# VectorE's 32x32 turns write adjacent elements with the channel outermost; TensorE reads runs and writes PSUM at a step

## What is computed

```python
def spectral_conv(x, w1, w2):
    x_ft = jnp.fft.rfft2(x)
    out_ft = jnp.zeros((b, w1.shape[1], h, w // 2 + 1), dtype=x_ft.dtype)
    out_ft = out_ft.at[:, :, :M1, :M2].set(jnp.einsum('bixy,ioxy->boxy', x_ft[:, :, :M1, :M2], w1))
    out_ft = out_ft.at[:, :, -M1:, :M2].set(jnp.einsum('bixy,ioxy->boxy', x_ft[:, :, -M1:, :M2], w2))
    return jnp.fft.irfft2(out_ft, s=(h, w))
h = layer_norm(x @ fc0_w + fc0_b, ln0_g, ln0_b)            # the stem
for i in range(LAYERS):                                     # 4 layers, M1 = M2 = 12
    x1 = spectral_conv(h, w1, w2)
    x2 = jnp.einsum('bchw,oc->bohw', h, conv_w[i]) + conv_b[i][None, :, None, None]
    h = layer_norm(x1 + x2, ln_g[i], ln_b[i])               # then gelu, but for the last layer
h = gelu(h @ fc1_w + fc1_b); h = gelu(h @ fc2_w + fc2_b); h = h @ fc3_w + fc3_b   # the head
```

## Time and profile before

| | us |
|---|---|
| median of three runs (lowest, highest) | 5721.86 (5716.95, 5734.56) |
| the profiled execution: its time, its span | 5729.41, 5727.7 |
| busy: TensorE, VectorE, ScalarE, GpSimd | 5285.1, 4230.7, 3896.4, 630.8 |
| mean granted TensorE clock | 0.967 of full |

### The profile page before, as it was taken

One profiled execution on the slowest core, in us unless ns is written; L12 is line 12 of the kernel. 1 busy time (PEld: TensorE's weight loads), 2 busy tenths in 40 slices (PEclk: granted clock), 3 DMA queues, 4 the chain that ended last, 5 costly groups with the idle time before them and its releaser, 6 DMA issues.

```text
span 5727.7 us, 135011 instructions
## 1 busy us (share of the span) xinstructions
PE 5285.1 (92%) x43556; PEld 2997.1 (52%) x43556; DVE 4230.7 (74%) x7712; ACT 3896.4 (68%) x6261; POOL 630.8 (11%) x943
## 2 busy tenths in 40 slices
PE   5887789999999999999999999999999999868778
PEld 2444456666666666666666654433333333334443
DVE  5888899999998999999999975555555555454553
ACT  5898776788666788666888656677777777523333
POOL 0133100233000233000233000000000000000000
PEclk9999999999999999999999999999999999877888
DMA  1334467667676667677676762221111111000000
GB/s 65 124 137 148 137 189 215 217 215 230 200 228 206 217 215 230 201 228 221 211 228 224 210 183 70 75 60 51 46 52 52 52 52 52 13 4 4 7 7 4
DMA packets 397185, 756.31 MB, mean 132 GB/s; under 512 B 245041, under 2 KB 303410, under 8 KB 331322
## 3 DMA queue, kind: packets, MB, share of 16 engines
q1 hardware_dynamic: 377402, 704.04, 38.8%
q0 software_dynamic: 19456, 48.01, 3.7%
HBM read 397.49 MB, written 354.42 MB: 131 GB/s over the span
## 4 chain that ended last, share of the span: by engine, by line
PE 81%; DVE 9%; issue 5%; ACT 3%; SPq 1%; DVEq 0%; ACTq 0%; DMA 0%
PE ps_y L914 18%; PE ps_y L907 9%; PE ps_t L926 9%; PE ps_t L1016 8%; PE ps_t L935 8%; PE ps_f L948 4%; PE ps_f L1001 3%; PE ps_s L893 3%; PE ps_f L986 3%; PE ps_s L961 3%; PE ps_t L1025 2%; PE ps_t L346 2%; PE ps_y L883 2%; ACT big L1169 1%; PE ps_f L336 1%
## 5 line engine op out<-in xcount | busy, mean ns | idle before, releaser
L1146 ACT ACTIVATE big<-ps_y 128x512 f32<-128x512 f32 x1280 | 777.0, 607 | 762.2 <-PE ps_y L914 699.6
L914 PEld LDWEIGHTS ps_y<-conv_now,big 128*128 128x128 f32 x8192 | 993.2, 191 | 520.2 <-issue 520.2
L1309 DVE TENSOR_REDUCE big<-big 128x16 f32<-128x512 f32 x1280 | 841.8, 679 | 522.5 <-ACT big L1146 522.3
L914 PE MATMUL ps_y<-conv_now,big 128*128 128x128 f32 x8192 | 1147.2, 283 | 0.0
L1302 DVE TENSOR_TENSOR big<-big 128x512 f32<-128x512 f32 x1280 | 932.1, 748 | 69.3 <-PE ps_t L926 62.2
L1155 ACT ACTIVATE big<-ps_t 128x512 f32<-128x512 f32 x1024 | 622.4, 608 | 334.2 <-PE ps_t L935 328.5
L926 PE MATMUL ps_t<-ident,big 128*128 128x128 f32 x5120 | 790.5, 277 | 43.9 <-DVE big L1302 42.5
L1162 ACT ACTIVATE big<-ps_t,g_now 128x512 f32<-128x512 f32 x1024 | 809.0, 790 | 9.3 <-PE ps_t L926 8.0
L1150 ACT ACTIVATE big<-ps_y 128x512 f32<-128x512 f32 x1280 | 780.1, 609 | 0.0
L926 PEld LDWEIGHTS ps_t<-ident,big 128*128 128x128 f32 x5120 | 587.6, 142 | 260.9 <-issue 204.8
L935 PE MATMUL ps_t<-ident,big 128*128 128x128 f32 x4096 | 654.4, 283 | 55.9 <-ACT big L1155 55.9
(11 more groups left out here) (180 smaller groups left out, 6419.0 us busy)
## 6 DMA issues: line engine op xcount, KB each, us to landing
hstore<-big SPq DMA_DIRECT2D x256, 1024.0 KB, 4.0
big<-hstore SPq DMA_DIRECT2D x256, 1024.0 KB, 5.3
xmodes<-x_out SPq DMA_DIRECT2D x128, 312.0 KB, 4.4
y_kt<-ymodes SPq DMA_DIRECT2D x512, 78.0 KB
ymodes<-y_st SPq DMA_DIRECT2D x192, 144.0 KB, 3.0
mix_room<-xmodes SPq DMA_DIRECT2D x48, 336.0 KB, 7.1
mix_room<-xmodes SPq DMA_DIRECT2D x48, 288.0 KB, 6.2
ymodes<-y_st SPq DMA_DIRECT2D x64, 192.0 KB, 3.4
```

Source lines behind the costliest of these rows:

```text
L914: last = mm(ps_y[:, wh, 128 * b:128 * b + 128], h_in[k // 2][:, at:at + 128], conv_now[:, :], start=False, stop=(b == 3))
L1146: af(y_sq[wh], ps_y[:, wh, :], ACT.Square).then_inc(s["sq_done"], 1)
L1309: v_.tensor_reduce(ss[:, k // 2, at:at + 16], groups(y_sq[wh]), AX.X, ALU.add).then_inc(s["ss_done"], 1)
```

## The change

The two turns write the turned block with the channel outermost: 32 (or 13 used of 32) places side by side for each channel, so each element is written beside the last. What they read from PSUM is as before, 32 floats apart. The matmuls that read their result walk it channel by channel, a run of 16 (or 13) adjacent elements and then a step to the next channel, and their output pattern is turned to match, so that each PSUM element gets the same value as before: consecutive results of one matmul now lie 32 floats (128 bytes) apart in PSUM. Which values are computed, all buffers, all waits and the order of instructions stay.

```diff
@@ inv_h @@
-                        mm(ps_y[64 * half:64 * half + 64, wh, :], c_inh[r, :], z_kx[j][r, 512 * odd:512 * odd + 512],
-                           start=True, stop=False)
+                        mm(ps_y[64 * half:64 * half + 64, wh, :].rearrange("p (w o) -> p o w", o=32), c_inh[r, :],
+                           z_kx[j][r, :].rearrange("p (o w) -> p o w", w=32)[:, :, 16 * odd:16 * odd + 16], start=True, stop=False)
@@ fwd_w @@
-                            last = mm(ps_s[at:at + 32, sx, 0:RUN], c_fww[r, :], t_w[r, j, 512 * sx:512 * sx + RUN],
+                            last = mm(ps_s[at:at + 32, sx, 0:RUN].rearrange("p (k c) -> p c k", c=32), c_fww[r, :],
+                                      t_w[r, j, :].rearrange("p (c k) -> p c k", k=32)[:, :, 16 * sx:16 * sx + KX],
                                       start=True, stop=True)
@@ turn_z @@
-                v_.transpose(z_kx[j].rearrange("p (w o) -> p o w", o=32), flat(of).rearrange("p (k o) -> p o k", o=32)
+                v_.transpose(z_kx[j].rearrange("p (o w) -> p o w", w=32), flat(of).rearrange("p (k o) -> p o k", o=32)
                              ).then_inc(s["iw_read"], 1)
@@ turn_w @@
-                v_.transpose(t_w[:, j, :].rearrange("p (k c) -> p c k", c=32), flat(ps_f).rearrange("p (w c) -> p c w", c=32)
+                v_.transpose(t_w[:, j, :].rearrange("p (c k) -> p c k", k=32), flat(ps_f).rearrange("p (w c) -> p c w", c=32)
                              ).then_inc(s["tw_done"], 1)
```

## The result

The changed kernel takes 5702.17 us (median of 7 runs, 5687.06 to 5708.09), the kernel before on the same chip 5732.31 us (7 runs, 5716.95 to 5736.59). The ratio is 0.9949, with a 95% interval from 0.9934 to 0.9965: 30 us faster, 0.5%. The profiled execution of the changed kernel took 5708.09 us with a span of 5706.4; that of before 5729.41 us with 5727.7. The two traces are thus 21.3 us apart.

What follows compares the result with a forecast made beforehand. TensorE was taken to bound the middle passes and head, no engine the stem. Turns give 23 us and TensorE pays 0: median 5721.9 - 23 = 5699 us, range 5680 to 5880.

Steps and rivals of the forecast that it cites:

- The turn's length: VectorE's turn_w and turn_z without the write step: about 1254 ns each, a saving of 0.73 us a turn.
- the prediction's estimate from them, 1.94 us: Turn time by the skill's SBUF stream figures if the PSUM source still hops as in SBUF: 1.94 us, no gain.
- TensorE untouched: inv_h and fwd_w keep their pace despite stepped PSUM writes, L907 at 613 ns and L961 at 523: cost 0.
- from below the price is 0: Lower bound of what inv_h and fwd_w pay on TensorE for the new access patterns: 0, against 612 us from above.
- the first rival: Stepped PSUM writes slow inv_h and fwd_w, 6066 to 6311 us; a small price could come from short runs; chance 0.32.
- The 23 us: Total gain on the chain: 32 turns, mostly in the stem, each ending 0.73 us earlier.
- pieces counted: Turns holding the chain for over 1 us: 28 between 105 and 806 us, four later, priced at 0.73 us each.
- the other 480 turns lie beside TensorE's matmuls and I cost them at nothing: Turns outside the 32 counted on the chain: covered by TensorE's own work, gain 0.
- Can the stem take 23 us? Yes: Between 300 and 560 us ScalarE comes next; some 10 turns give 7 us, less than its 24 us of idle time.
- the 374 foreseen: Fall of VectorE's busy time in us, 512 turns at 0.73 us, to some 3860.
- The wait of L987: TensorE's wait at the mixing for turn L1290: from 1.8 us each down to 1.1.
- the turn did not stay: Second rival: the PSUM read sets the turn's pace, so its length stays and TensorE pays nothing; 5722 us; chance 0.24.

Runs made afterwards that it cites:

- run 11: Changed kernel with turn_w reading PSUM side by side and writing 128 bytes apart, the mirror of the change; 5723.48 us, one run.
- Runs 5 and 6: Changed kernel with the experts' first matmul on bf16, first writing to adjacent places, then 128 bytes apart in PSUM; 5653.39 and 5690.86 us, one run each.
- run 2: Kernel before with only turn_z and inv_h changed; 5729.45 us, ratio 0.9990 to the kernel before.
- run 3: Changed kernel with GpSimd's addition of mirrored weights cut from 576 columns to 12; 5684.99 us, ratio 0.9931 to the kernel before.
- run 9: Changed kernel with the first of GpSimd's two weight additions in a quad moved ahead of its copy of the modes; 5684.9 us, ratio 0.9919.
- run 4: Kernel before with GpSimd's addition of mirrored weights cut from 576 columns to 12; 5722.27 us, ratio 0.9990.
- run 10: On top of run 9, ScalarE's second sign pass (sign_w2) moved behind the squares, so both additions should come early; 5732.57 us, ratio 1.0005.
- 12: Kernel before, with long turns, and GpSimd's first weight addition moved ahead of its copy of the modes; 5726.23 us, ratio 0.9994.

## Why the prediction was right, and where its steps were not

**The turn's length: right.** 1254 ns foreseen, 1227 to 1249 measured, and run 11 shows the reason that was only chosen there: the write step is the whole of the 0.73 to 0.76 us. The trace has 1.23 us with a source that still steps in PSUM. The figures of the Trainium skill, "Vector Engine (DVE) Microarchitecture Reference", section 5.2, are for SBUF streams, and the prediction's estimate from them, 1.94 us, does not carry over to a source in PSUM.

**TensorE untouched: right, but for a little in `fwd_w`, and the stated reason fits.** `inv_h` 613 ns before and after; its call still holds the chain for 1.02 us in the middle of the changed kernel, as in the earlier trace rows, and `fwd_w` for 1.44 us in place of 1.38 to 1.39. In the chain of the changed kernel (start us, us, what):

```profile
2502.74 1.02 PE ps_y L907 x8
...
2514.42 1.19 PE ps_s L961 x10
...
2515.62 0.01 PE ps_s L961
...
2515.75 0.24 PE ps_s L961 x4
```

The step "from below the price is 0" missed 8 ns of the median record of `fwd_w` (509 to 517), the small price that the first rival had named for its rows of 13; rows of 16 and 32 are free here. With 96 of the 128 calls in the middle passes at 0.05 us this is 5 us at most; 1.5 were lost there. The Trainium skill, "Advanced Engine Details and Errata", section "PSUM Cachelines", was the first rival's ground. Runs 5 and 6 agree with it for bf16 (379 to 602 ns), this kernel's fp32 matmuls do not (613 to 613).

**The 23 us: right in sum, wrong in its parts, and the sum in part by luck.** The prediction counted pieces of the chain, at 0.73 us each. By stretch it foresaw, and got (in the one pair of traces, and by the means of three and six):

```
stretch             pieces counted   foreseen   one pair   means
ahead of quad 8            1            0.7       10.8      11.7
quads 8 to 23             16           11.7        3.9       1.9
mixing quads              11            8.0        8.4      12.4
stem                      28           20.4       23.1      26.0
middle and after           4            2.9       -1.5 (middle)
```

No stretch came as worked out, unless it is the mixing quads in the one pair; TensorE's waits there for the turn, between 600 and 830 us, fell from 22.4 to 23.4 us in the long-turn traces to 11.2 to 13.4 in the short-turn ones, since the waits got fewer as well as shorter. The two large errors go in opposite directions and about cancel, which is luck. Two steps failed.

The first is "the other 480 turns lie beside TensorE's matmuls and I cost them at nothing". That holds for the middle passes and for `turn_z` (run 2). It does not hold in quads 1 to 7, where both turns of a quad hold `normed`, though the chain gives the turn a small piece and books the rest as "issue". The chain of the kernel before at one such turn:

```profile
128.00 0.66 DVE big L1289
...
128.90 0.90 issue
129.80 0.68 DVE big L1302
```

The turn runs for 1.95 us and `normed` is queued behind it on VectorE; no semaphore ends that wait, so it has no releaser. Seven quads with two turns at 0.73 us are 10.2 us, and 10.8 came, but that match is in part chance: TensorE's 14 waits for `normed` fell from 14.9 us in all (80 to 238 us, before) to 7.1 (80 to 227.7, changed), which is 7.8 us. The other 3 go with TensorE's granted clock, which rose in the same stretch from 0.95 to 0.99 of 2.4 GHz; that this is what paid them is argued. In 80 to 230 us, before and after:

```profile
80.00:230.00 150.00, 123.16 (x1076) 69.62 (x1076) 126.23 (x256) 123.07 (x225) 10.43 (x21) 0.95 0.32 117
```

```profile
80.00:230.00 150.00, 129.09 (x1148) 72.09 (x1148) 126.63 (x276) 131.92 (x244) 10.43 (x21) 0.99 0.33 125
```

The second is "Can the stem take 23 us? Yes". I asked for ScalarE's idle time, and not who runs beside the operations that follow the turn. The 16 counted pieces were to give 11.7 us; 1.9 to 3.9 came. What took the place of the turn's tail is GpSimd's addition. The timeline of the kernel before:

```profile
409.27 2.02 DVE L1289 STREAM_TRANSPOSE big<-ps_f 128x1024 f32<-128x1024 f32 x1
...
410.29 1.86 POOL L816 TENSOR_TENSOR wslot<-wslot,w_raw 128x576 f32<-128x576 f32 x1
...
411.09 2.21 DVE L1302 TENSOR_TENSOR big<-big 128x512 f32<-128x512 f32 x2
```

In the changed kernel:

```profile
417.21 1.21 DVE L1290 STREAM_TRANSPOSE big<-ps_f 128x1024 f32<-128x1024 f32 x1
...
418.22 1.81 POOL L816 TENSOR_TENSOR wslot<-wslot,w_raw 128x576 f32<-128x576 f32 x1
418.34 2.83 DVE L1303 TENSOR_TENSOR big<-big 128x512 f32<-128x512 f32 x2
...
420.63 1.12 PE L926 MATMUL ps_t<-ident,big 128*128 128x128 f32 x4 [0.33 <-DVE big L1303]
...
421.67 2.08 PE L883 MATMUL ps_y<-big 49*128 49x512 f32 x4
```

Two `normed` take 2.83 us beside the addition and 1.25 undisturbed. In the kernel before, about half of the addition lies beside the last part of the turn, which reads one operand, from PSUM, and keeps its 2.02 us; only the rest holds `normed`, 2.21 us. From the start of the turn to the end of the two `normed` it is 4.03 us before and 3.96 after, so 0.07 us is left of the 0.8 by which this turn got shorter.

TensorE waits for the first `normed`; what it then issues runs at the slower of its two levels, 1.2 GHz (granted clock 0.50 in 420.6 to 423.6 us): the same four L926 take 1.12 us for 0.60 to 0.66, the four L883 2.08 for 1.13. In 300 to 560 us the changed kernel has a granted clock of 0.94, run 3 one of 0.99, and run 9 0.97. The windows of the changed kernel and of run 3:

```profile
300.00:560.00 260.00, 211.72 (x1762) 116.86 (x1760) 213.28 (x419) 236.59 (x419) 98.03 (x139) 0.94 0.42 144
```

```profile
300.00:560.00 260.00, 211.81 (x1863) 117.76 (x1864) 209.31 (x441) 248.27 (x444) 68.26 (x152) 0.99 0.44 153
```

With TensorE busy for as long, run 3 gets more done, and that is why I think runs 3 and 9 gave more than expected. The additions alone do not set this clock: in run 4, with the additions short and the turns long, it is 0.92. How much of what the additions take back is the hold and how much the clock is not separated.

The Trainium skill, "SBUF — State Buffer", section "SBUF: two separate sides", states a rule for this: of a VectorE operation with two SBUF inputs and a GpSimd operation that reads SBUF, the one that starts first holds the shared access for its whole length, and the other waits. The trace agrees: 2.83 us is the 1.25 of two `normed` and nearly the 1.81 of the addition. That the addition is what holds `normed`, and no coincidence of place, is what runs 3, 4, 9, 10 and 12 show; they shorten the addition or move it.

The same collisions stand in the middle passes (two `normed` take 2.87 us at 1206.72 in the changed kernel, 2.18 at 1230.31 before), but TensorE's own work hides them there. They are also a part of why VectorE's busy time fell by 252.6 us and not by the 374 foreseen. The records of the turns got 382 us shorter, those of `normed` 76 longer and those of `sums` 11; no other group of VectorE moved by more than 0.1. The last 42 or so were never free: a record overlaps the next one, a long turn by 0.15 to 0.20 us (128.00 + 1.95 against 129.80, 409.27 + 2.02 against 411.09) and a short one by 0.08 (417.21 + 1.21 against 418.34), and busy time counts that once. 42 us over 512 turns are 0.08 us each, about that difference. From its own start to the start of the next operation a turn thus got some 0.67 us shorter (1.80 to 1.13 in these rows), where the prediction priced it at 0.73.

**The rest.** The wait of L987 fell from 1.8 us each to 1.25, not to 1.1, and there are four fewer. The forecast was 5699 for a kernel before of 5721.9; that kernel then measured 5732.3 beside the changed one. Taken as differences it is 23 us foreseen against 30 measured, and 21 between the two profiled executions; the interval of the ratio, 20 to 38 us, holds 23. The stem's marks, as means of several traces, give 26. So 5702 came 3 us from 5699 because a gain some 7 us larger and a base 10 us higher made up for each other. Neither rival's main mechanism acted: the PSUM step costs fp32 nothing, and the turn did not stay.

**What stays open.** The stem has more to give than run 9 takes: in run 3 `normed` has a mean of 673 ns over the whole kernel, in run 9 704. Whether the second addition can lie beside one-input work too, without the delay of `sign_w2` that undid run 10, was not tried. What a higher granted clock gives by itself, ahead of quad 8 and behind a held `normed`, was not separated from the waits, and neither was the pace of a matmul from its type in what a stepped write costs.

## What to carry to other kernels

In these runs a step cost VectorE's turn at its SBUF write and not at its PSUM read, and TensorE at its moving read and not at the PSUM write of an fp32 matmul; the PSUM write of a bf16 matmul did pay. So a layout's step is best moved to the fp32 matmul's output. When an operation on an in-order engine gets shorter, what follows moves earlier and meets other neighbours, so look for two-input VectorE work that will now lie beside a GpSimd operation, and place that one under one-input work. In a chain, an "issue" piece behind a short piece of a long operation can be the wait for that operation, as at 128.90 us here: look at the engine's timeline before pricing it at nothing. And read a stage's gain from several traces of kernels that are alike in that stage; here one pair was off by up to 4 us in a stretch.

## What the runs showed of the hardware that was not expected

- A PSUM write at a 128-byte step costs a bf16 matmul of 512 results 223 ns (379 to 602). It costs an fp32 matmul of 512 results nothing (613 to 613), and one of 416 nothing at 64 bytes (509 to 509).
- A moving operand read at a 128-byte step costs an fp32 record of 512 columns 427 ns (613 to 1040); rows of 13, read and written, cost 8 ns in 509, rows of 16 nothing.
- VectorE's 32x32 turn out of PSUM: 1227 ns with a stepped read, 1988 with a stepped write, 1986 with both.
- A VectorE operation with two SBUF inputs that starts behind GpSimd's addition of 1.8 to 1.9 us lasts until that has ended, however short it is: 225 ns became 1774. Turns and copies from PSUM beside the same addition kept their 1.21, 1.04 and 0.69 us.
